# A reordered opening for a cross-attention and mixed-expert layer: keys and values of the first batch ahead of the first queries

## What is computed

```python
def layer(x, ctx):                       # x (16, 112, 256), ctx (16, 375, 256)
    q = (layernorm(x) @ w_q + b_q)       # split in 16 heads of 16
    k, v = split(ctx @ w_kv + b_kv)
    a = softmax(q @ k.T * 0.25)          # per batch and head
    x = x + (a @ v) @ w_out + b_out
    h = layernorm(x)
    g = mean over batches of gate(h)     # (112, 8)
    y = relu(sum_e g_e (h @ W1_e.T) + g @ b1)
    return x + sum_e g_e (y @ W2_e.T) + g @ b2
```

## Time and profile before

| | |
|---|---|
| median of 3 runs | 951.06 us (950.96 to 954.01) |
| profiled execution | 955.64 us, its span 953.6 us |
| PE busy | 901.2 us, 95% of the span |
| DVE, ACT, POOL busy | 467.8, 244.7, 236.1 us |
| PE busy from 95 to 265 us of the span | 164.96 of 170 us |
| PE busy from 0 to 10, 10 to 20, 20 to 30, 30 to 40, 40 to 50 us | 0.00, 3.63, 9.03, 6.72, 9.30 us |

### The profile page before, as it was taken

One profiled execution on the slowest core, in us unless ns is written; L12 is line 12 of the kernel. 1 busy time (PEld: TensorE's weight loads), 2 busy tenths in 40 slices (PEclk: granted clock), 3 DMA queues, 4 the chain that ended last, 5 costly groups with the idle time before them and its releaser, 6 DMA issues.

```text
span 953.6 us, 17240 instructions
## 1 busy us (share of the span) xinstructions
PE 901.2 (95%) x6250; PEld 747.1 (78%) x6250; DVE 467.8 (49%) x799; ACT 244.7 (26%) x453; POOL 236.1 (25%) x365
## 2 busy tenths in 40 slices
PE   2888999999987899999999999999999999999998
PEld 2766888888865688888888888878888888888887
DVE  6676778777774465555555555543331112111121
ACT  2646777777755200000000001012211001000000
POOL 6443555555513214111111111312203003000000
PEclk9899999999998999999999999999999999999999
DMA  7469776767740370010001000201002001000000
GB/s 188 99 160 237 191 171 179 171 182 182 195 104 9 99 265 23 22 44 22 22 22 44 22 22 22 88 23 43 24 23 89 0 1 45 0 0 3 25 22 28
DMA packets 43799, 74.10 MB, mean 78 GB/s; under 512 B 12379, under 2 KB 33963, under 8 KB 43763
## 3 DMA queue, kind: packets, MB, share of 16 engines
q1 hardware_dynamic: 43762, 73.61, 28.0%
HBM read 56.41 MB, written 17.01 MB: 77 GB/s over the span
## 4 chain that ended last, share of the span: by engine, by line
PE 84%; DMA 5%; DVE 3%; ACT 2%; issue 2%; POOL 2%; SPq 2%; ACTq 0%; POOLq 0%; DVEq 0%
PE banks L308 40%; PE banks L1513 32%; PE banks L1250 3%; PE banks L1232 3%; PE banks L1209 3%; DMA k_stack<-k_dram 3%; DMA w_f<-in_wv 1%; PE banks L1495 1%; DMA k_dram<-k_parts 1%; ACT probs L696 1%; DVE x_norm L1002 1%; DVE maxima L971 1%; POOL k_parts L575 1%; PE banks L1261 1%; SPq L378 0%
## 5 line engine op out<-in xcount | busy, mean ns | idle before, releaser
L308 PE MATMUL banks<-w_parts,xt_parts 128*128 128x512 f32 x1344 | 305.8, 390 | 0.0
L308 PEld LDWEIGHTS banks<-w_parts,xt_parts 128*128 128x128 f32 x1344 | 252.1, 188 | 53.6 <-issue 1.1
L1513 PE MATMUL banks<-w_parts,h_high 128*128 (+1 forms) x896 | 240.9, 391 | 1.6 <-DVE h_low L1129 1.6
L1098 DVE SCALAR_TENSOR_TENSOR acc<-banks,gates,acc 128x512 f32<-128x512 f32 x196 | 147.1, 751 | 119.4 <-PE banks L308 119.4
L1513 PEld LDWEIGHTS banks<-w_parts,h_high 128*128 128x128 f32 x896 | 167.4, 188 | 35.7 <-DVE h_low L1129 1.8
L594 POOL TENSOR_TENSOR w_parts<-w_raw,w_parts 128x1024 fp32r<-128x1024 f32 (+1 forms) x32 | 76.4, 2394 | 416.2 <-ACT w_parts L733 416.2
L1123 DVE SCALAR_TENSOR_TENSOR y<-banks,gates,y 128x256 f32<-128x256 f32 x112 | 54.2, 484 | 235.7 <-PE banks L1513 231.4
L1513 PE MATMUL banks<-w_parts,h_low 128*128 (+1 forms) x448 | 138.2, 390 | 0.0
L971 DVE TENSOR_REDUCE maxima<-banks 112x2 f32<-112x750 f32 x128 | 117.6, 934 | 27.0 <-PE banks L1209 24.2
L733 ACT ACTIVATE w_parts<-w_raw 128x1024 fp32r<-128x1024 f32 (+1 forms) x32 | 33.6, 1058 | 354.6 <-PE banks L308 261.0
L696 ACT ACTIVATE probs<-banks 128x448 f32<-128x448 f32 x192 | 100.2, 544 | 23.0 <-PE banks L1232 20.9
(11 more groups left out here) (112 smaller groups left out, 738.0 us busy)
## 6 DMA issues: line engine op xcount, KB each, us to landing
w_raw<-in_w SPq DMA_DIRECT2D x32, 512.0 KB, 3.3
k_dram<-k_parts SPq DMA_DIRECT2D x16, 576.0 KB, 3.1
k_stack<-k_dram SPq DMA_DIRECT2D x32, 288.0 KB, 3.8
k_stack<-k_dram SPq DMA_DIRECT2D x32, 192.0 KB, 4.1
c_raw<-in_ctx_t SPq DMA_DIRECT2D x16, 375.0 KB, 3.8
k_stack<-k_dram SPq DMA_DIRECT2D x32, 96.0 KB, 4.4
b_rows<-gate_dram SPq DMA_DIRECT2D x12, 256.0 KB, 4.5
q_dram<-q_parts SPq DMA_DIRECT2D x16, 168.0 KB, 4.3
```

The costliest lines, as they stand in the source:

```text
L308: last = pe.matmul(out_ap, left(a, k), right(b, k), start=(n == 0), stop=(n == 3 * tiles - 1))
L1098: dve.scalar_tensor_tensor(out=acc[:, t, 512 * s:512 * s + 512], in0=banks[:, t % NB1, :], scalar=gate_col, in1=base[:, 512 * s:512 * s + ...
L1513: last = pe.matmul(banks[:, t % 2, :], h_part[a][:, t, 2 * c + k, :], w, start=(n == 0), stop=(n == 3 * OT - 1))
```

## The change

SyncE loads the context of batch 0 and the key weights directly behind the first group of queries. PE projects the keys of batch 0 (both halves), transposes the first queries, projects the values of batch 0, and only then projects the first queries; each later group's transpose is put ahead of the projection before it. DVE makes the low part of context 0, which POOL made; the statistics of groups 2 and 3 stand behind the normalisation of group 1. POOL makes `key_rest(0)` between the roots of group 0 and of group 1 and `key_third(0)` between these and those of groups 2 and 3. The count `w_high_done` becomes one semaphore for each weight.

```diff
@@ SyncE
             load_x(0)
-            load_w(WQ, wq)
-            load_x(1)
             sp.wait_ge(pad_set, 1)
             load_context(Batch(0))
             load_w(WK, wk)
+            sp.dma_start(small_sb[:], small).then_inc(small_loaded, 16)
+            load_w(WQ, wq)
+            load_x(1)
+            load_w(WV, wv)
             load_x(2)
             load_x(3)
-            sp.dma_start(small_sb[:], small).then_inc(small_loaded, 16)
             load_context(Batch(1))
-            load_w(WV, wv)
@@ GpSimd
             inverse_root(0, GB, 0)
-            context_low(Batch(0))
+            key_rest(Batch(0))
             pool.wait_ge(bits_halved, 2)
             inverse_root(GB, 2 * GB, ROOT_OPS)
+            key_third(Batch(0))
             pool.wait_ge(bits_halved, 3)
             inverse_root(2 * GB, B, 2 * ROOT_OPS)
+            query_rest(0)
             context_low(Batch(1))
-            key_rest(Batch(0))
-            query_rest(0)
-            key_third(Batch(0))
@@ ScalarE
             act.wait_ge(pad_set, 1)
-            weight_high(WQ)
             context_high(Batch(0))
             weight_high(WK)
-            context_high(Batch(1))
+            weight_high(WQ)
+            act.wait_ge(small_loaded, 16)
+            key_copy(Batch(0), 0)
+            key_copy(Batch(0), 1)
+            key_first(Batch(0))
+            query_high(0)
             weight_high(WV)
-            query_high(0)
-            act.wait_ge(small_loaded, 16)
+            value_evac(Batch(0), 0, 2)
+            value_evac(Batch(0), 2, 1)
             for m in range(2):
-                key_copy(Batch(0), m)
-                if m == 1:
-                    key_first(Batch(0))
                 query_evac(0, m)
             query_high(1)
+            context_high(Batch(1))
             query_high(2)
-            value_evac(Batch(0), 0, 2)
-            value_evac(Batch(0), 2, 1)
@@ VectorE
             query_stats([0])
+            dve.wait_ge(c_high_done, 1)
+            dve.tensor_tensor(c_low[:, 0], c_raw[:, 0], c_high[:, 0], ALU.subtract).then_inc(c_low_done, 1)
+            weight_low(WK)
             weight_low(WQ)
+            query_norm(0)
             query_stats([1])
-            query_norm(0)
-            weight_low(WK)
-            query_stats([2, 3])
+            key_second(Batch(0))
             query_low(0)
             weight_low(WV)
-            for g in range(1, NG):
-                query_norm(g)
-                if g == 2:
-                    key_second(Batch(0))
+            query_norm(1)
+            query_stats([2, 3])
+            query_norm(2)
             query_low(1)
             query_parts(0)
+            query_norm(3)
             query_low(2)
+            query_parts(1)
             query_low(3)
-            query_parts(1)
@@ TensorE
-            query_transpose(0)
             pe.wait_ge(w_low_done[WK], 1)
             for m in range(2):
                 key_project(Batch(0), m)
-                if m == 0:
-                    pe.wait_ge(w_low_done[WQ], 1)
-                query_project(0, m)
-            query_transpose(1)
-            query_transpose(2)
+            query_transpose(0)
             pe.wait_ge(w_low_done[WV], 1)
             pe.wait_ge(ones_set, 2)
             for c in range(CH):
                 value_project(Batch(0), c)
+            pe.wait_ge(w_low_done[WQ], 1)
+            for m in range(2):
+                query_project(0, m)
+            query_transpose(1)
             for g in range(1, NG):
+                if g < NG - 1:
+                    query_transpose(g + 1)
                 for m in range(2):
                     query_project(g, m)
-                if g == 1:
-                    query_transpose(3)
```

More of the change, by code:

```diff
@@ L256, in build @@
         stack_set, pad_set = sem("stack_set"), sem("pad_set")
-        w_high_done = sem("w_high_done")
+        w_high_done = [sem(f"w_high_done{n}") for n in range(5)]
         w_low_done = [sem(f"w_low_done{n}") for n in range(5)]
@@ L667, in weight_high @@
                 act.wait_ge(w_loaded[n], 16)
-                act.activation(w_high[:, n], w_f32[:, n], ACT.Copy).then_inc(w_high_done, 1)
+                act.activation(w_high[:, n], w_f32[:, n], ACT.Copy).then_inc(w_high_done[n], 1)
             def query_high(g):
@@ L960, in weight_low @@
             def weight_low(n):
-                dve.wait_ge(w_high_done, n + 1)
+                dve.wait_ge(w_high_done[n], 1)
                 dve.tensor_tensor(w_low[:, n], w_f32[:, n], w_high[:, n], ALU.subtract).then_inc(w_low_done[n], 1)
```

## The result

The changed kernel takes 957.53 us (median of 16 runs), the kernel before 952.68 us beside it; the ratio is 1.0045 with a 95% interval of 1.0029 to 1.0061. By the ratio it is slower by 4.3 us (2.8 to 5.8; the two medians differ by 4.85), where +4.5 was forecast. The 955.6 us of the forecast started from 951.06 for the kernel before, which came out at 952.68 in this comparison. The profiled execution's span is 956.6 us against 953.6.

What follows compares the result with a forecast made beforehand. No single engine owns the opening's chain; a delay of the first reduction carries to the end. Key weights −3.7, but twelve matmuls 3.6 later and swapped order 1.0: +4.6, rounded to +4.5, 955.6 us against 951.06; range 949.8 to 958.2.

Steps and rivals of the forecast that it cites:

- Loads and keys: Opening, batch 0: key weights land at 8.3 against 12.03, `key_rest` ends at 18.3 against 28.6, used by nothing sooner.
- The roots: POOL and DVE: group 1's root ends at 22.1, late statistics at 28.5, second root at 32.6 against 22.1.
- The clash: Group 2's normalisation on DVE, from 32.6, meets two POOL instructions: 1.6 plus twice 1.1 to 1.2 us, until 36.5.
- my 1.1 to 1.2 us for each: Extra DVE time for each large POOL instruction running beside group 2's four normalisations: 1.1 to 1.2 us.
- The projection of group 1: PE's twelve matmuls begin at 38.1 against 34.54, take 4.85 us at low clock; `query_rest(1)` starts at 44.2.
- the rival of the same time: Group 1's twelve matmuls run at high clock, about 2.4 us: +2.2, 953.2 us; chance 0.20, smaller terms included.
- The end of the opening: DVE's list from `bv_wide` to the first reduction takes 6.4 us as before; reduction at 55.3, 4.6 later.
- The 1.0 us for the order of `query_parts(1)` and `query_low(3)`: DVE's list: `query_parts(1)` now stands ahead of `query_low(3)` and both wait for `query_rest(1)`; adds 1.0 us.
- the case that the prediction put aside as just beginning to matter: PE's last projection of queries falls to the low clock in the gap and ends 2.4 us later, at 55.4.
- The carrying: From the first reduction on every step feeds the next, so its delay of 4.6 us carries to the end.
- the rival of a delay taken back: Stack loads at 75.56 may be held by traffic, so a later reduction costs nothing: 951 us; chance 0.09.

Runs made afterwards that it cites:

- e6: Changed kernel with SyncE's load order of the kernel before; 1.0094 of the kernel before, 4.7 us above the changed kernel.
- e1: Changed kernel with the statistics of groups 2 and 3 back ahead of group 1's normalisation on DVE; 1.0010 of the kernel before.
- e5: Kernel before with one edit, the statistics of groups 2 and 3 behind group 1's normalisation on DVE; 1.0055 of the kernel before.
- e9: Changed kernel with context 0's low part on POOL behind the root of group 0; 1.0107 of the kernel before.
- e10: Changed kernel with context 0's low part on POOL ahead of the root of group 0; 1.0067 of the kernel before.
- e3: Changed kernel with `query_low(3)` ahead of `query_parts(1)` on DVE; 1.0058 of the kernel before.

## Why the prediction was right, step by step

**Loads and keys.** The context landed at 5.62 (5.9 was taken), and ACT reached the key weights at 7.65 without waiting (8.3). `key_rest` ended at 17.77 (18.3). The load order is worth 4.7 us in the new order, in which the queries hang on the keys (e6). That the early keys bring nothing by themselves fits e1, which has them and is level with the kernel before; no run puts the early loads alone into that kernel.

**The roots.** Group 1's root ended at 21.96 (22.1), its normalisation at 24.65 (24.8), the statistics at 28.22 (28.5), the second root at 31.87 (32.6; it took 3.57 us undisturbed, and 4.05 in the earlier trace rows). e1 and e5 show this step as the cause from both sides: taken out of the changed kernel it gives back 3.3 us, put into the kernel before it costs 5.2 (3.2 to 7.3).

**The clash.** The normalisation of group 2 took 4.64 us where I said 3.9. The first of its four instructions alone took 3.67, until both POOL instructions were over (31.83 to 35.43), by the view of this tile (ns min/median/max, first and last start):

```profile
L941 DVE TENSOR_SCALAR xq<-x_all,mean_var,rstd x4: 399/400/3672, 31.9 to 36.1; 112x256 f32<-112x256 f32 x4
```

That is the exclusion for the whole instruction as the Trainium skill states it (SBUF — State Buffer, Who interferes with whom); my 1.1 to 1.2 us for each came from a case in which DVE was already under way. This miss (+0.7) and the shorter root (−0.7) cancel by luck: the twelve matmuls began at 38.04 (38.1).

**The projection of group 1.** From the start of the first to the end of the last the twelve matmuls took 3.6 us (38.04 to 41.63; the chain gives them 3.29), not 4.85. The granted clock was 0.50 until past 39.4, and the last half ran at the high level, with pairs of 448 columns at 0.57 us for 0.95. So `query_rest(1)` started at 42.91 (44.2). Half of the rival of the same time did come true here, although PE's gap was 8.8 us and not 6. Which half is chance: the same matmuls behind the same eight transposes took 3.9 us in e6, 4.2 in e9, 4.5 in e10 and 4.8 in e3, as the clock rose earlier or later in them. The profile of the changed kernel happens to be the shortest of the five. Whether the transposes have a part in the rise, no run parts.

**The end of the opening.** The 1.0 us for the order of `query_parts(1)` and `query_low(3)` lies within the 0.4 to 1.6 that the profiles give it (under e3), but part of it is another term than the one in my sum. It was the case that the prediction put aside as just beginning to matter: PE, idle for 2.8 us until `query_low(3)`, fell to the low level, and the projection of group 3 and the first keys of batch 1 ran there. By the stretches of the changed kernel (us, PE busy, granted clock, DMA share, GB/s; the first holds the eight transposes and the first matmuls of group 1, the second the projection of group 3):

```profile
34.50:39.40 4.90, 2.80 (x12) 0.50 0.00 0
47.60:52.30 4.70, 4.65 (x13) 0.50 1.06 230
```

The twelve matmuls from 47.65 took 4.65 us instead of the 2.5 in my sum, and the first reduction waited 1.13 us for PE. In e6, e9 and e10, with the same gap of 2.8 us, these matmuls took 3.9 to 4.1 us and the reduction came straight behind DVE's list, so that the wait is that of one profile in four. It came at 54.47 for 55.3, a shift of 3.7 instead of 4.6: the projection of group 1 was 1.3 us shorter than in the sum, and the rest of the way 0.5 longer.

**The carrying.** The same 3.7 us stand at the landmark; the rival of a delay taken back is refuted up to there, and the 4.3 us of the ratio agree within their interval (2.8 to 5.8). The mechanism is borne out; that the forecast of 4.5 lies 0.2 us from the measured time is luck in part, since terms of up to 1.3 us in the sum were off with both signs. Over all twelve kernels the first reduction and the landmark move together, to within about 1.5 us of the distance in the kernel before; the time follows them less closely (e5: 8.0 in the profile, 5.2 in the median; e9: 3.0 over the changed kernel, and 5.9). One profile is one execution, and e5's was its slowest; what else sets these differences stays open.

## What to carry to other kernels

When an order is changed so that one strand goes first, list for every in-order engine what now stands behind the new waits: here the strand that gained 10 us fed nothing that was waited for sooner, while statistics that nothing held back stood behind an instruction that waited for it. Work that is ready and feeds a long serial chain on another engine (thirteen small instructions, 3.6 us) belongs ahead of work that waits. And after such a step, look at which large POOL instruction meets which SBUF-to-SBUF instruction of DVE: moving the high and low parts of one context made a tie into 3 us of gain, with the clock as a possible helper.

## What the runs showed of the hardware that was not expected

Small POOL instructions are stretched as well: beside DVE's `c_low` (two inputs in SBUF, 0.94 us) an instruction of 0.20 us took 0.81 at 7.96. The root of group 0 thus ended at 11.66, where it ended at 10.47 before. DVE waited 1.77 us for it, but not on the chain that ended last.

And POOL instructions that follow each other without a gap may let no DVE instruction in between them. In the changed kernel this was so for two (3.67 us, above). In e5 three of them ran from 30.77 to 35.94, and one DVE instruction of 0.40 us that started at 30.85 took 5.24:

```profile
L942 DVE TENSOR_SCALAR xq<-x_all,mean_var,rstd x4: 399/400/5235, 30.8 to 36.7; 112x256 f32<-112x256 f32 x4
```

Here their cost to DVE is the sum of their lengths. It is not always so. In the rows of e3 above DVE's second `w_low` (two inputs in SBUF) took 2.40 us, until 0.6 us behind the end of `query_rest(2)`, and the `context_low(2)` that followed on POOL without a gap took 2.25 us instead of 1.77 to 1.83: DVE went in between the two, and POOL waited. What decides it is not shown. The cost is smaller where they are spread over instructions of DVE that read PSUM: the first reduction of the changed kernel, beside `query_rest(3)`, kept its 0.94 us.
